# Three row normalisations from VectorE to ScalarE, with the shift made on GpSimd and a bias folded into a product

## The chip, the cores and the metric

The kernel runs on one core of a Trainium2 chip. Five engines work side by side, each with its own queue of instructions in a fixed order: TensorE (PE, with its weight loads as PEld), VectorE (DVE), ScalarE (ACT), GpSimd (POOL) and SyncE (SP), which issues most DMAs. They meet through semaphores: an instruction waits until a counter has reached a value. The metric is device time in microseconds (us) for one execution, as the median of the runs shown.

## The reference

Two blocks in a row, on 16 sequences of 256 tokens with 128 features, all fp32. The first is a state-space ("mamba") block with a residual and a row normalisation; the second is two transformer layers with attention in windows of 64 and a gated feed-forward; a residual and a last row normalisation follow. Cut to what matters here:

```python
# block 1
u = silu(conv(x @ in_w + in_b)); delta = softplus((u @ dt1_w + dt1_b) @ dt2_w + dt2_b)
h = A_bar * h + Bu            # scan over 256 tokens, 16 states, 256 channels
y = (einsum(hs, C_mat) + D_vec * u) * silu(x @ gate_w + gate_b)
x = _layernorm(x + y @ out_w + out_b)                 # normalisation 1
# block 2, for each of two layers
q, k, v = split(shift_token(x) @ wqkv)                # then l2norm, rotary, windows, softmax
x = x + o @ wo
h = shift_token(x)
h = (h - mu) / sqrt(var + 1e-05) * lg + lb            # normalisation 2
a, g = split(h @ w1 + b1)
x = x + (a * gelu(g)) @ w2 + b2
# end: residual with the input of block 2, then
out = _layernorm(x + ...)                             # normalisation 3
```

## The kernel before

The 32 row tiles of 128 tokens are worked in 10 groups (`SIZES`), four groups of two tiles and six of four tiles. A group passes through block 1 (index `g`) and then twice through block 2 (index `f` counts the 20 pairs of layer and group in the order `QUAD`, index `q` the 64 single tiles in it). Work on several groups is interleaved: while the scans of group g run, tiles of earlier groups go through attention and feed-forward.

Nothing is scheduled at run time. Each engine has a table of steps (`PE_ORDER`, `ACT_ORDER`, `DVE_ORDER`, `POOL_ORDER`, `SP_ORDER`), and runs them in that order. A step such as `ffn_norm 13` is a small function that waits on semaphores and issues a few instructions. Two further tables (`PAIR_TABLES`, `BANK_TABLES`) give the PSUM banks (AA, BB, YY in pairs, C and M single) that each step uses.

The three normalisations have the same shape, here for a group of two or four tiles:

- the statistics are made on DVE (`bn_stats`, `bn_aggr`, one pair for each tile), which give mean and variance of each row: steps `mamba_sum` (lines 1115 and 1120), `ffn_stats` (1205, 1210) and `final_stats` (1115, 1120);
- `mamba_rstd`, `ffn_rstd` and `final_rstd` on POOL add epsilon (line 774) and raise to the power -0.5 (line 776);
- `mamba_norm` and `final_out` (line 1125) and `ffn_norm` (line 1220) on DVE subtract the mean and multiply by the result, one `tensor_scalar` of 128x128 for each tile. Over the whole kernel these are 32 + 64 + 32 = 128 instructions in 40 steps.

Who waits for them: after `mamba_norm` PE transposes the rows (`layer_T`), after `ffn_norm` PE transposes (`norm_T`), ACT applies gain and offset of the layer (`norm_T` on ACT, line 957), and the up products follow; after `final_out` SP stores the group. `outb`, the tile in which a group's output is summed and normalised, exists once, so that `ffn_sum` of the second layer waits until the store of the group before has landed.

The bias of the down product is not in the product. The step `residual` on POOL adds it to the rows `x2` (line 812), and in the second layer adds the rows `x1` as well (line 815); `ffn_sum` on DVE then adds the product and waits for both.

`mamba_norm`'s DVE instruction, and the two POOL lines of the residual:

```python
ins = dve.tensor_scalar(dst[:, i, :], src[:, i, :], mv[:, i, 0:1], rs[:, i:i + 1],
                        ALU.subtract, ALU.mult)
pool.tensor_tensor(rows, rows, row("b2", g, l), ALU.add).then_inc(xb2_sb, 1)
pool.tensor_tensor(rows, rows, x1[:, g % X_RING, 0:tiles_of(g)], ALU.add).then_inc(xb1_sb, 1)
```

## Time and profile before

| what | value |
|---|---|
| median of three runs | 1025.17 us (1023.71 to 1028.51) |
| the profiled execution, device time | 1025.69 us |
| its span, first to last instruction | 1023.9 us |
| mean granted TensorE clock | 0.979 |
| busy PE / DVE / ACT / POOL | 906.2 / 890.3 / 788.3 / 701.1 us |

The profile gives for each engine the time in which at least one of its instructions ran. Matmuls overlap each other, and so do short ACT and DVE instructions that follow each other, so a sum of single durations can exceed the busy time. An engine's idle time is split by what ended it: the last semaphore that it waited for, or "issue" where the trace shows no such wait. The span is shorter than the device time of the same execution by 1.8 us.

### The profile page before, as it was taken

Reading aid. Unit: us, or ns where it says so; the run is one execution under the profiler, and the core shown is the slowest. Engines: PE = TensorE matmul, PEld = TensorE weight load, DVE = VectorE, ACT = ScalarE, POOL = GpSimd, SP = SyncE. Lnnn points to the kernel's source line nnn. Section 1 sums busy time; section 2 is a strip of 40 time slices with the busy share of each in tenths; the row PEclk is TensorE's granted clock in tenths of the full one; section 3 lists DMA queues with packets and bytes.
Section 4 is the critical chain, followed back from the end, with each engine's and each line's share of the span. In section 5 each row is a group of like instructions: output and inputs, shape, how many; then the busy total and the mean of one; then the engine's idle time right before and its main releaser. Section 6 shows DMA issues by size and latency. Waiting matters only on the chain. (4 is left out here: it accounts for less than half of the span.)

```text
span 1023.9 us, 26019 instructions
## 1 busy us (share of the span) xinstructions
PE 906.2 (89%) x10152; PEld 550.7 (54%) x10152; DVE 890.3 (87%) x1244; ACT 788.3 (77%) x1901; POOL 701.1 (68%) x386
## 2 busy tenths in 40 slices
PE   3767678999988898999899989999899999999985
PEld 1333335456455465646564555546565566676664
DVE  7798997999879997999899998999899997774643
ACT  4467766996888859977898759995987987778771
POOL 4062424998579984799588892999478497886651
PEclk9979889999999999999999999999999999999998
DMA  7000000000001100000101100100110000010000
GB/s 239 11 17 16 12 1 21 23 19 15 17 17 27 27 23 16 18 22 22 32 18 27 22 12 22 28 23 6 28 32 23 2 23 22 17 33 18 17 22 11
DMA packets 22618, 25.63 MB, mean 25 GB/s; under 512 B 2869, under 2 KB 14815, under 8 KB 22495
## 3 DMA queue, kind: packets, MB, share of 16 engines
q1 hardware_dynamic: 22207, 23.81, 9.0%
q8 instruction: 81, 1.33, 0.6%
q14 instruction: 42, 0.34, 0.1%
q10 hardware_dynamic: 288, 0.14, 0.0%
HBM read 9.26 MB, written 2.10 MB: 11 GB/s over the span
## 5 line engine op out<-in xcount | busy, mean ns | idle before, releaser
L1088 DVE TENSOR_TENSOR_SCAN scan<-du,decay 128x1028 f32<-128x1028 f32 (+1 forms) x160 | 315.0, 2004 | 2.8 <-issue 1.3
L793 POOL TENSOR_TENSOR rn<-ssc,expo 128x16 f32<-128x16 f32 x64 | 214.6, 3354 | 5.3
L884 ACT ACTIVATE decay<-delta,negA 128x1024 f32<-128x1024 f32 (+1 forms) x160 | 154.9, 997 | 43.3 <-DVE scan L1088 37.7
L1278 PE MATMUL YY<-scan,diag 64*64 64x512 f32 (+1 forms) x1280 | 148.1, 552 | 32.1 <-DVE scan L1088 31.7
L789 POOL TENSOR_SCALAR ssc<-ss 128x16 f32<-128x16 f32 x64 | 61.9, 967 | 152.7 <-DVE ss L1145 152.0
L798 POOL TENSOR_TENSOR qkc<-qkc,qks 128x1024 f32<-128x1024 f32 x64 | 163.0, 2547 | 0.5 <-DVE qks L1163 0.3
L802 POOL TENSOR_TENSOR qkc<-qkc,rn 128x1024 f32<-128x1024 f32 x64 | 143.5, 2242 | 5.0
L940 ACT ACTIVATE prob<-AA,nmax 128x128 f32<-128x128 f32 x240 | 84.5, 384 | 15.1 <-DVE nmax L1183 15.0
L940 ACT ACTIVATE prob<-BB,nmax 128x128 f32<-128x128 f32 x232 | 81.7, 381 | 17.3 <-DVE nmax L1183 14.9
L1145 DVE TENSOR_REDUCE ss<-sq 128x16 f32<-128x1024 f32 x64 | 77.2, 1206 | 15.1 <-ACT sq L903 15.1
L1278 PEld LDWEIGHTS YY<-scan,diag 64*64 64x64 f32 x1280 | 38.3, 139 | 94.5 <-DVE scan L1088 68.9
L1278 PE MATMUL BB<-wqkv,hT 128*128 128x512 f32 x124 | 60.5, 610 | 3.7 <-ACT hT L895 1.8
L1278 PE MATMUL AA<-wqkv,hT 128*128 128x512 f32 x112 | 54.9, 613 | 6.4 <-ACT hT L895 2.0
L940 ACT ACTIVATION_READ_ACCUMULATOR prob<-AA,nmax 128x1 f32 x240 | 53.7, 224 | 0.0
L1278 PEld LDWEIGHTS M<-v_even,probT 128*64 128x64 f32 x640 | 41.2, 140 | 20.8 <-issue 16.8
L940 ACT ACTIVATION_READ_ACCUMULATOR prob<-BB,nmax 128x1 f32 x232 | 51.2, 221 | 0.0
L1278 PE MATMUL M<-v_even,probT 128*64 128x64 f32 x640 | 46.6, 227 | 1.6 <-ACT v_odd L919 1.4
L1278 PE MATMUL M<-v_odd,probT 128*64 128x64 f32 x640 | 46.7, 228 | 0.0
L903 ACT ACTIVATE sq<-BB 128x512 f32<-128x512 f32 x62 | 35.8, 616 | 11.3 <-PE BB L1278 10.9
L1052 DVE SCALAR_TENSOR_TENSOR hu<-upre,pv,hu 128x512 f32<-128x512 f32 (+1 forms) x60 | 42.2, 704 | 2.1
L1278 PEld LDWEIGHTS C<-wo,oT 128*128 128x128 f32 x352 | 40.4, 192 | 6.5 <-issue 4.2
L1278 PE MATMUL C<-wo,oT 128*128 128x128 f32 x352 | 42.3, 277 | 1.8 <-DVE x L1245 1.5
(210 smaller groups left out, 2279.2 us busy)
## 6 DMA issues: line engine op xcount, KB each, us to landing
v_even<-v_odd SPq DMA_DIRECT2D x96, 128.0 KB, 2.3
x<-in_x SPq DMA_DIRECT2D x6, 256.0 KB, 3.3
wqkv<-in_wqkv SPq DMA_DIRECT2D x1, 1536.0 KB
xT<-in_xT SPq DMA_DIRECT2D x6, 256.0 KB, 2.7
out<-outb SPq DMA_DIRECT2D x6, 256.0 KB, 2.3
w<-in_w SPq DMA_DIRECT2D x1, 682.0 KB
xT<-in_xT SPq DMA_DIRECT2D x4, 128.0 KB, 2.5
x<-in_x SPq DMA_DIRECT2D x4, 128.0 KB, 2.9
```

The lines of the kernel that those rows point to most:

```text
L789: pool.tensor_scalar(ssc[:, :], ss[:, :], 1e-24, None, ALU.max).then_inc(ssc_sb, 1)
L793: pool.tensor_tensor(rn[:, q % 2, :], ssc[:, :], expo[:, 0:2 * HEADS], ALU.pow).then_inc(rn_sb, 1)
L798: pool.tensor_tensor(both_qk, both_qk, qks[:, q % 2].rearrange("p a x -> p (a x)"), ALU.add).then_inc(rope_add, 1)
L802: pool.tensor_tensor(all_heads, all_heads, rn[:, q % 2, :].unsqueeze(2).to_broadcast((P, 2 * HEADS, DH)), ALU.mult).then_inc(qk_sb, 1)
L884: act.activation(decay[:, at % A_RING, both(g), 1:], delta[:, both(g), :], ACT.Exp, scale=negA[:, n:n + 1]).then_inc(decay_sb, 1)
L903: act.activation(sq[:, a, :], bank_of("qk_in", q, a), ACT.Square).then_inc(sq_sb, 1)
L940: ins = act.activation(prob[:, h, :], bank_of("scores", q, a)[:, c * P:(c + 1) * P], ACT.Exp, bias=nmax[:, q % 2, h:h + 1], accum_out=den[ ...
L1052: dve.scalar_tensor_tensor(out=hu[:, ab(g, h), :], in0=upre[:, ab(g, h), c:c + SEQ], scalar=col("conv_w", k + c), in1=hu[:, ab(g, h), :], ...
L1088: dve.tensor_tensor_scan(state, step, a, 0.0, ALU.add, ALU.mult).then_inc(scan_sb, 1)
L1145: dve.tensor_reduce(ss[:, :], sq[:, :, :].rearrange("p a (h x) -> p (a h) x", x=DH), AX.X, ALU.add).then_inc(ss_sb, 1)
L1278: return pe.matmul(dst, lhsT, rhs, start=start, stop=stop, skip_group_check=True)
```

## The change

The three normalisations leave DVE and become ScalarE activations of the kind `Identity`, `scale * x + bias`, with scale and bias read from a column for each row. The scale is the power from POOL as before. The bias is -mean * scale, for which POOL makes two more small instructions in every `rstd` step (lines 782 and 786 of the changed kernel). `mamba_norm`, `ffn_norm` and `final_out` so stand in ACT's order and no longer in DVE's. The bias of the down product becomes row 86 of the third chunk of `w2`, against a row of ones in `hid`, and the third matmul of each tile contracts over 86 rows and no longer 85; `residual` keeps only the addition of `x1` in the second layer. All five order tables and both bank tables are written anew. The diff, cut to its core:

```diff
-for _name, _n in (("A_log", NST), ("out_b", D), ("qk_scale", LAYERS * 2 * DH), ("b2", LAYERS * D)):
+for _name, _n in (("A_log", NST), ("out_b", D), ("qk_scale", LAYERS * 2 * DH)):
...
-                             (w2[0:CH[2][1], :, 2, :], t["w2"][:, 2 * P:HID, :].rearrange("l p n -> p l n"))]:
+                             (w2[0:CH[2][1] + 1, :, 2, :], t["w2"][:, 2 * P:HID + 1, :].rearrange("l p n -> p l n"))]:
...
+            pool.memset(hid[:, NCH - 1, :], 1.0)
...
-            def rstd(dst, mv, ve, g, nth, aggr, var, done):
+            def rstd(dst, off, mv, ve, g, nth, aggr, var, done, used, left):
                 n = tiles_of(g)
                 pool.wait_ge(aggr, nth)
                 pool.tensor_scalar(ve[:, 0:n], mv[:, 0:n, 1], EPS, None, ALU.add).then_inc(var, 1)
+                if nth > 1:
+                    pool.wait_ge(used, nth - 1)
+                pool.tensor_scalar(off[:, 0:n], mv[:, 0:n, 0], -1.0, None, ALU.mult).then_inc(left, 1)
                 pool.wait_ge(var, nth)
-                pool.tensor_tensor(dst[:, 0:n], ve[:, 0:n], expo[:, 0:n], ALU.pow).then_inc(done, 1)
+                pool.tensor_tensor(dst[:, 0:n], ve[:, 0:n], expo[:, 0:n], ALU.pow).then_inc(left, 1)
+                pool.wait_ge(left, 2 * nth)
+                pool.tensor_tensor(off[:, 0:n], off[:, 0:n], dst[:, 0:n], ALU.mult).then_inc(done, 1)
...
-                pool.tensor_tensor(rows, rows, row("b2", g, l), ALU.add).then_inc(xb2_sb, 1)
-                if l == 1:
-                    pool.wait_ge(xb2_sb, f + 1)
-                    pool.tensor_tensor(rows, rows, x1[:, g % X_RING, 0:tiles_of(g)], ALU.add).then_inc(xb1_sb, 1)
+                pool.tensor_tensor(rows, rows, x1[:, g % X_RING, 0:tiles_of(g)], ALU.add).then_inc(xb1_sb, 1)
...
+            def normalise(dst, src, of, rs, g, sig):
+                for i in range(tiles_of(g)):
+                    ins = act.activation(dst[:, i, :], src[:, i, :], ACT.Identity, bias=of[:, i:i + 1], scale=rs[:, i:i + 1])
+                ins.then_inc(sig, 1)
+            def ffn_norm(f):
+                l, g = QUAD[f]
+                act.wait_ge(f_rstd, f + 1)
+                if f:
+                    act.wait_ge(hnT_ps, f)
+                normalise(hn, tiles(one("shift", f)[:, :]), f_of, f_rs, g, hn_sb)
...
-            def normalise(dst, src, mv, rs, g, sig):
-                for i in range(tiles_of(g)):
-                    ins = dve.tensor_scalar(dst[:, i, :], src[:, i, :], mv[:, i, 0:1], rs[:, i:i + 1],
-                                            ALU.subtract, ALU.mult)
-                ins.then_inc(sig, 1)
...
                 dve.wait_ge(f_stat, f + 1)
+                if f:
+                    dve.wait_ge(f_rstd, f)
...
                 dve.wait_ge(w2_ps, f + 1)
-                dve.wait_ge(xb2_sb, f + 1)
...
+                        n += c == NCH - 1
...
 DVE_ORDER = """
-differences 0, masks 0, step_size 0, tables 0, scan 0 0, scan 0 1, scan 0 2, scan 0 3, scan 0 4, scan 0 5, scan 0 6,
+differences 0, step_size 0, scan 0 0, scan 0 1, scan 0 2, scan 0 3, scan 0 4, scan 0 5, scan 0 6, masks 0, scan 0 7,
```

Three places show what the new tables do. The first is ACT at the end of group 0's scans: `decay` is a scan's input, `upre` the first product of group 1 (for the convolution on DVE), `hT` the transposed rows of group 0. Before:

```order
L884 ACTIVATE decay<-delta,negA 128x2x256 x16
L844 ACTIVATE upre<-YY,pv 128x256 x2
L894 ACTIVATE hT<-C 64x256
L895 ACTIVATE hT<-C 64x255
L859 ACT_TABLE_LOAD
```

and now:

```order
L891 ACTIVATE decay<-delta,negA 128x2x256 x16
L961 ACTIVATE x<-x,m_of,m_rs 128x128 x2
L851 ACTIVATE upre<-YY,pv 128x256 x2
L901 ACTIVATE hT<-M 64x256
L902 ACTIVATE hT<-M 64x255
L866 ACT_TABLE_LOAD
```

The two normalising instructions of group 0 stand ahead of `upre` of group 1 in ACT's queue.

The second is POOL at its end, from the next to last group's feed-forward: `f_` names belong to normalisation 2, `z_` names to normalisation 3. Before:

```order
L774 TENSOR_SCALAR z_ve<-z_mv 128x2
L776 TENSOR_TENSOR z_rs<-z_ve,expo 128x2
L774 TENSOR_SCALAR f_ve<-f_mv 128x2
L776 TENSOR_TENSOR f_rs<-f_ve,expo 128x2
L812 TENSOR_TENSOR x<-x,bv 128x256
L815 TENSOR_TENSOR x<-x 128x256
L774 TENSOR_SCALAR z_ve<-z_mv 128x2
L776 TENSOR_TENSOR z_rs<-z_ve,expo 128x2
```

and now:

```order
L779 TENSOR_SCALAR f_ve<-f_mv 128x2
L782 TENSOR_SCALAR f_of<-f_mv 128x2
L784 TENSOR_TENSOR f_rs<-f_ve,expo 128x2
L786 TENSOR_TENSOR f_of<-f_of,f_rs 128x2
L779 TENSOR_SCALAR z_ve<-z_mv 128x2
L782 TENSOR_SCALAR z_off<-z_mv 128x2
L784 TENSOR_TENSOR z_rs<-z_ve,expo 128x2
L786 TENSOR_TENSOR z_off<-z_off,z_rs 128x2
L822 TENSOR_TENSOR x<-x 128x256
```

Each power has got a negation ahead of it and a product behind it, the addition of the bias is gone, and the statistics of group 8's output are now worked behind those of group 9's last feed-forward.

The third is ACT at its end; `hnT` and `hid` belong to the feed-forward, `outb` to the output. Before:

```order
L957 ACTIVATE hnT<-C,pv 128x256
L966 ACTIVATE hid<-YY,pv 128x256 x2
L966 ACTIVATE hid<-M,pv 85x256
```

and now:

```order
L961 ACTIVATE hn<-M,f_of,f_rs 128x128 x2
L984 ACTIVATE hnT<-C,pv 128x256
L995 ACTIVATE hid<-AA,pv 128x256 x2
L995 ACTIVATE hid<-M,pv 85x256
L961 ACTIVATE outb<-outb,z_off,z_rs 128x128 x4
```

The four `outb` instructions are those of groups 8 and 9, two each; group 8's output is normalised behind the last gelu. On DVE before, group 8's output was normalised ahead of the last feed-forward's statistics. Over the whole program ACT has 58 table loads before and 55 now.

## Rows read from the trace of the kernel before

**Rows 1.** The page's part 1: busy time, share of span, instructions.
```profile
PE 906.2 (89%) x10152; PEld 550.7 (54%) x10152; DVE 890.3 (87%) x1244; ACT 788.3 (77%) x1901; POOL 701.1 (68%) x386
```
**Rows 2.** Stretches: start:end, length, busy of PE, PEld, DVE, ACT, POOL (instructions); clock, DMA.
```profile
0.00:200.00 200.00, 140.66 (x1295) 70.44 (x1296) 176.22 (x230) 133.21 (x258) 82.80 (x55) 0.92 0.15 44
200.00:850.00 650.00, 610.13 (x7012) 369.94 (x7011) 609.56 (x804) 538.70 (x1309) 508.36 (x252) 1.00 0.08 21
...
850.00:1000.00 150.00, 142.11 (x1781) 100.66 (x1779) 96.36 (x182) 113.82 (x332) 105.65 (x72) 0.99 0.09 22
...
400.00:500.00 100.00, 96.69 (x1091) 58.83 (x1091) 93.01 (x121) 81.23 (x199) 86.70 (x40) 1.00 0.09 21
```
**Rows 3.** PE's waits from 200 to 850 us: for whom, us, times, longest.
```profile
PE YY L1278 <- DVE scan L1088: 6.0, 6, 2.1
PE BB L1419 <- ACT prob L940: 3.3, 6, 1.2
```
**Rows 4.** ACT's longest wait in the same stretch.
```profile
ACT prob L940 <- DVE nmax L1183: 24.2, 13, 5.5
```
**Rows 5.** DVE's groups by line: busy us, mean ns, idle before and its releaser.
```profile
L1125 DVE TENSOR_SCALAR x<-x,m_mv,m_rs 128x128 f32<-128x128 f32 x32 | 14.2, 499 | 3.7 <-POOL m_rs L776 3.7
...
L1220 DVE TENSOR_SCALAR hn<-C,f_mv,f_rs 128x128 f32<-128x128 f32 x38 | 13.0, 399 | 0.4 <-POOL f_rs L776 0.4
...
L1125 DVE TENSOR_SCALAR outb<-outb,z_mv,z_rs 128x128 f32<-128x128 f32 x32 | 12.8, 457 | 1.3 <-POOL z_rs L776 1.3
...
L1220 DVE TENSOR_SCALAR hn<-M,f_mv,f_rs 128x128 f32<-128x128 f32 x26 | 8.9, 400 | 1.9 <-POOL f_rs L776 1.9
```
**Rows 6.** Line 1125 alone from 200 to 850 us: DVE busy (instructions).
```profile
200.00:850.00 650.00, 20.55 (x42) 1.00 0.08 21
```
**Rows 7.** Line 1220 alone in the same stretch.
```profile
200.00:850.00 650.00, 14.92 (x44) 1.00 0.08 21
```
**Rows 8.** Single durations on line 1125, ns: shortest/median/longest.
```profile
L1125 DVE TENSOR_SCALAR x<-x,m_mv,m_rs x32: 296/341/2248, 45.2 to 862.3; 128x128 f32<-128x128 f32 x32
```
**Rows 9.** ACT's groups by line and shape.
```profile
L966 ACT ACT_TABLE_LOAD x19 | 24.4, 1283 | 4.7 <-PE BB L1278 3.0 <-PE YY L1278 0.8 <-PE AA L1278 0.5
...
L966 ACT ACTIVATE hid<-BB,pv 128x256 f32<-128x256 f32 x10 | 4.2, 471 | 0.1
...
L957 ACT ACTIVATE hnT<-C,pv 128x256 f32<-128x256 f32 x6 | 3.6, 601 | 10.4 <-PE C L1504 10.4
...
L864 ACT ACTIVATE dt_s<-YY,pv 128x128 f32<-128x128 f32 x4 | 1.5, 382 | 0.9 <-PE YY L1278 0.9
```
**Rows 10.** POOL's groups by line.
```profile
L812 POOL TENSOR_TENSOR x<-x,bv 128x512 f32<-128x512 f32 (+1 forms) x20 | 26.9, 1347 | 24.5 <-DVE hn L1220 24.5
...
L774 POOL TENSOR_SCALAR f_ve<-f_mv 128x4 f32<-128x4 f32 (+1 forms) x20 | 9.3, 467 | 45.5 <-DVE f_mv L1210 44.8
```
**Rows 11.** Timeline after group 0's scans: start, duration, what [idle before].
```profile
44.12 0.84 ACT L844 ACTIVATE upre<-YY,pv 128x256 f32<-128x256 f32 x2 [6.81 <-PE YY L1278]
...
45.15 0.60 DVE L1125 TENSOR_SCALAR x<-x,m_mv,m_rs 128x128 f32<-128x128 f32 x2 [1.14 <-POOL m_rs L776]
...
45.67 0.41 DVE L1048 TENSOR_SCALAR hu<-upre,pv 128x256 f32<-128x256 f32 x1
```
**Rows 12.** Timeline of the last 17 us.
```profile
1007.67 0.22 POOL L774 TENSOR_SCALAR f_ve<-f_mv 128x2 f32<-128x2 f32 x1 [1.70 <-DVE f_mv L1210]
1007.98 0.72 POOL L776 TENSOR_TENSOR f_rs<-f_ve,expo 128x2 f32<-128x2 f32 x1
1008.73 0.73 DVE L1220 TENSOR_SCALAR hn<-M,f_mv,f_rs 128x128 f32<-128x128 f32 x2 [1.14 <-POOL f_rs L776]
...
1013.82 0.47 ACT L966 ACTIVATE hid<-M,pv 85x256 f32<-85x256 f32 x1 [0.38 <-PE M L1278]
...
1018.11 0.42 DVE L1245 TENSOR_TENSOR outb<-M,x 128x256 f32<-128x256 f32 x1 [1.70 <-PE M L1278]
...
1020.48 0.60 DVE L1125 TENSOR_SCALAR outb<-outb,z_mv,z_rs 128x128 f32<-128x128 f32 x2 [1.14 <-POOL z_rs L776]
```

More of the change, by code:

```diff
@@ L782, in mamba_rstd @@
             def mamba_rstd(g):
-                rstd(m_rs, m_mv, m_ve, g, g + 1, m_aggr, m_var, m_rstd)
+                rstd(m_rs, m_of, m_mv, m_ve, g, g + 1, m_aggr, m_var, m_rstd, x1_sb, m_left)
             def scale(q):
@@ L1117, in stats @@
                 dve.wait_ge(stat, n)
+                if g:
+                    dve.wait_ge(rstd, g)
                 dve.memset(tick[:, :], 0.0)
```

555 lines of the change are left out of this document (275 added, 280 removed).

## The prediction, made before the changed kernel had run

> **What bounds the kernel now.** I read the busy times first. Over the span PE is busy 906.2 us and DVE 890.3 us, ACT 788.3 us and POOL 701.1 us [rows 1], but an average over 1023.9 us hides that the limits change, so I cut the span into stretches [rows 2]. The reader is to compare, in each row, the length with the busiest engine. From 0 to 200 us DVE is busy 176 us and PE only 141: the first groups run through scans with little else to do, and DVE sets the pace. From 200 to 850 us PE (610.1) and DVE (609.6 of 650 us) are level at 94%, ACT is at 83% and POOL at 78%. From 850 to 1000 us the scans are over; PE is at 95% and DVE at 64%. The last 24 us are one chain from engine to engine. So a load taken off DVE pays fully in the first stretch, partly in the second, where PE has only 39.9 us of idle to give back, and not in the third.
>
> Then I asked whom PE waits for in the second stretch. The longest entry is the scan on DVE with 6.0 us, the next the softmax exponentials on ACT with 3.3 us [rows 3]; no single cause comes near the 39.9 us. It is idle in many small pieces, from both engines. ACT in turn waits there for DVE's row maxima, 24.2 us [rows 4], which DVE reaches late because its queue is full.
>
> **The change, part by part.**
>
> *DVE loses the 128 normalising instructions.* Their busy time is 14.2 + 13.0 + 12.8 + 8.9 = 48.9 us [rows 5], of which 20.55 + 14.92 = 35.5 us lie from 200 to 850 us, in 42 + 44 = 86 instructions [rows 6, 7]. In the first 200 us fall the eight tiles of groups 0 to 2 and the first four of the feed-forward; at 0.30 and 0.37 us a tile (0.60 us for two [rows 11], 0.73 us for two [rows 12]) that is 3.9 us. The remaining 9 us or so lie behind 850 us, beside a DVE with room.
>
> One part of the 35.5 us is less sure than it looks. The normalisations that read SBUF take 0.30 us at the shortest and 2.25 us at the longest [rows 8], while those that read PSUM have a mean of 0.40 us [rows 5]; something holds the first kind up at times. Undisturbed, the 64 of them would be 64 x 0.30 = 19 us and not 27.0 us. If the hold-up passes to the next DVE instruction, 8 us of the 48.9 us, and some 6 us of the 35.5 us, are not saved.
> The Trainium skill says why this could be so (page "SBUF — State Buffer", section "Who interferes with whom"): VectorE and GpSimd share one pair of ports, the one that issues second blocks for the whole instruction of the other, and that holds for a tensor_scalar in a two-port mode as for any VectorE instruction with two SBUF inputs, which the scan is. By this rule the lower saving is the right one, and by the row alone the full one. The trace agrees in that only the form that reads SBUF has the long cases [rows 5, 8].
>
> *ACT gains them.* No row shows an Identity of 128x128 with both a scale and a bias from a column. The nearest: one column operand at this size takes 382 ns, and a second column operand costs 601 - 471 = 130 ns at 128x256 [rows 9]. That gives 512 ns for one. Two that follow each other overlap: two upre of 0.47 us take 0.84 us [rows 11], so each further one in a step adds 0.10 us less, 412 ns. With 24 steps of four tiles at 1.75 us and 16 of two at 0.92 us the sum is 42.0 + 14.8 = 57 us. If the second operand costs nothing it is 24 x 1.23 + 16 x 0.66 = 40 us. I take 57, since the row with both operands is the nearest kind; 86/128 of it, 38 us, comes in the second stretch. The new table has three table loads less, 3 x 1.28 = 3.8 us [rows 9], some 2.6 us of it there. ACT in the second stretch then has 538.7 + 38 - 2.6 = 574 us of work. DVE has 609.6 - 35.5 = 574 us as well, and PE still 610 us. The change so levels ACT and DVE below PE.
>
> *POOL* loses the 20 bias additions, 26.9 us, and gains 80 small instructions, between 0.22 us [rows 12] and 0.467 us [rows 10] each, 18 to 37 us. With 508 of 650 us busy [rows 2] this changes nothing as load. It does as delay: the negation stands between epsilon and power, and the product behind the power waits for it. From the gap of 0.09 us between two POOL instructions that depend on each other [rows 12] I get 0.25 us for the first and 0.31 us for the second, 0.55 us on each normalisation's way. It can be twice that in the second stretch (0.467 us in place of 0.22 us), where PE has other work in its queue.
>
> *PE* contracts over 86 rows where it had 85, in the same number of matmuls with the same columns: zero. What ffn_sum no longer waits for is an addition that was ready long before: zero. The new waits of the statistics for the rstd step of the group before, and of POOL for ACT's last normalisation, concern steps a group old: zero. The row of ones is one memset at the start, beside PE's wait for its weights: zero. On DVE the masks and tables move from ahead of the first scan to between scans. It is the same work on the same engine before the same last scan, so I take zero, though it may close or open an idle time of a microsecond or two.
>
> *Start.* Now the order counts. ACT normalises group 0 ahead of upre of group 1. Before, upre came at 44.12 us, while the normalisation on DVE ran only at 45.15 us, when the power was there; the convolution followed at 45.67 us [rows 11]. Now upre stands behind a wait until 45.15 + 0.55 = 45.7 us and 0.92 us of normalising, and the convolution, which needs the first half of upre, starts near 47.1 us: 1.4 us later, on DVE's path. For groups 1 and 2 upre stands ahead. The start gains 3.9 - 1.4 = 2.5 us; I take 2.
>
> *End.* The chain of the last group passes two normalisations. Each is later by 0.55 us on POOL and by 0.92 us on ACT against 0.73 and 0.60 us on DVE [rows 12]: 0.74 + 0.87 = 1.6 us. Group 8's output now stands behind the last gelu, which ends at 1014.29 us; normalised at 1015.2 us and stored in the 2.8 us that the last store takes (from 1021.08 us, the end of the last row of [rows 12], to the span's end at 1023.9), it frees outb at 1018.0 us, just ahead of the sum that needs it at 1018.11 us. Zero, up to 0.5 us.
>
> *Middle.* Between nothing and all of the idle time. With the load as it is PE reaches 96.7% in its best 100 us [rows 2]; at that share 610.1 us of work take 631 us, a gain of 19 us. This is one bound, and zero is the other. I take about half, 10 us (PE at 95.3%), because DVE gives up 35.5 us but ACT, which PE waits for nearly as often as for DVE [rows 3], takes 38 us.
>
> **The sum.** -2 - 10 + 0 + 1.6 = -10.4 us against the profiled execution, 1025.69 us: 1015.3 us. Its time lies 0.5 us above the median of the runs shown, so 1015 us against 1025.2 us.
>
> **The rivals.**
> 1. *DVE was the true limit.* PE's gaps are the echo of a DVE that is never free: the 24.2 us that ACT waits for row maxima [rows 4] speak for it. Then PE fills to 96.7% and the middle gives 19 us: -2 - 19 + 1.6, 1006 us. Against it: PE's own waits for DVE are few [rows 3].
> 2. *PE is the limit and nothing is hidden behind DVE.* The middle stays at 650 us; -2 + 1.6 gives 1025 us. For it: level busy times at 94% [rows 2], idle in small pieces. The new bank tables may also shift the small pieces either way.
> 3. *ACT's queue becomes the limit, slower.* ACT has 111 us of idle in the second stretch, 24.2 us of it waits for one result of DVE [rows 2, 4]. If such waits are latencies that stay, and do not shrink as work is added, the 36 us of net work lengthen the stretch, in the worst case in full. It decides as soon as less than 36 us of the 111 can be filled; with a third of the added work uncovered the middle grows by 12 us, and the time is 1037 us. The place is ACT's order, in which a normalisation waits for POOL with exponentials and copies for PE queued behind it, as in the start above.
>
> **How the numbers follow.** The forecast, 1008 to 1020 us, gets 0.40. Rival 1 gets 0.20, rival 2 0.24, rival 3 0.16. A measurement of this kernel can tell about 0.5%, 5 us, from no change. Faster by more (below 1020 us) are the forecast and rival 1: 0.60. Within it (1020 to 1030 us) is rival 2: 0.24, and slower is rival 3: 0.16. For a range that holds 8 times in 10 I cut the outer part of rival 1 and the outer half of rival 3: 1001 to 1034 us.
>
> **What would show it.** In the profile of the changed kernel: DVE busy near 841 us if the hold-ups go, 849 us if they pass on; ACT near 841 us; the new activations near 0.41 to 0.51 us; PE near 906 us, with its share in the middle at 95%. The convolution of group 1 should start about 1.4 us later than before relative to the statistics of group 0, and the last normalisation about 1.6 us later relative to the last attention output. I am wrong if PE's share in the middle stays at 94% or if ACT's activations turn up at the top of PE's waits. A middle that shrinks by over 19 us would say that PE's best stretch was no bound.

## The result, and the profile of the changed kernel

The changed kernel takes 1055.12 us (median of four runs, 1054.6 to 1055.62) against 1026.84 us (1023.71 to 1029.07) for the kernel before: a ratio of 1.0278, 95% interval 1.0245 to 1.031. It is slower by 2.8%. I had forecast 1015 us, with 1034 us as the upper end.

The page's part 1 of the changed kernel, under [rows 1]:

```profile
PE 927.4 (88%) x10152; PEld 556.6 (53%) x10152; DVE 839.4 (80%) x1116; ACT 826.3 (78%) x2026; POOL 690.2 (65%) x447
```

Set against [rows 1], the work itself moved almost as forecast: DVE lost 50.9 us, ACT gained 38.0 us, POOL lost 10.9 us. The span is 1053.8 us, 29.9 us longer. Of these PE is busy for 21.2 us and idle for 8.7 us. Its instructions are the same 10152. In the kernel before 36.4 us of PE's busy time lie at the lower of TensorE's two clock levels (1.2 GHz, half of 2.4 GHz), in the changed one 72.8 us. At half speed half of the difference, 18 us, is lost, so 18 of the 21.2 us are slower matmuls. The stretches of the changed kernel, in the columns of [rows 2], show where:

```profile
0.00:200.00 200.00, 148.56 (x1266) 70.48 (x1266) 158.13 (x213) 132.36 (x255) 85.47 (x62) 0.85 0.15 43
200.00:850.00 650.00, 598.25 (x6722) 360.42 (x6722) 565.64 (x694) 545.12 (x1348) 477.69 (x280) 0.98 0.08 20
850.00:1000.00 150.00, 143.21 (x1775) 98.43 (x1775) 96.40 (x157) 120.49 (x349) 107.24 (x80) 1.00 0.09 21
400.00:500.00 100.00, 89.15 (x908) 52.51 (x907) 86.64 (x75) 75.65 (x179) 78.20 (x34) 0.96 0.09 21
```

The middle row is the one to read. In the same 650 us PE gets through 6722 instructions where it had got through 7012: 4% less of the kernel is done. Its share is 92%, not the 95% I wanted to see. DVE fell from 94% to 87%. ACT went from 538.7 to 545.1 us only, because less of the kernel fits in. Between them no engine is now busier than 92%. The granted clock is 0.98 there against 1.00, and 0.85 against 0.92 in the first 200 us. A mean of 0.85 means 30% of the stretch at the lower level.

Who waits for whom in the middle, ACT's longest entry (as [rows 4]) and PE's longest ones (as [rows 3]):

```profile
ACT prob L947 <- DVE nmax L1204: 23.5, 16, 5.0
```
```profile
PE AA L1425 <- ACT prob L947: 4.2, 5, 1.6
PE BB L1425 <- ACT prob L947: 3.6, 2, 2.8
PE C L1284 <- ACT oT L957: 2.9, 4, 0.9
PE AA L1284 <- ACT hnT L984: 2.7, 4, 1.1
```

ACT's wait for DVE's row maxima was 24.2 us and is 23.5 us, though DVE is busy 44 us less in the stretch (some 35 us of that are the normalisations, and less of the kernel fits in). And ACT now heads PE's list, where the scan on DVE had stood with 6.0 us. It does so with its exponentials, not with the new activations.

The new activations, ACT's groups by line (busy us, mean ns of one, idle before):

```profile
L961 ACT ACTIVATE hn<-M,f_of,f_rs 128x128 f32<-128x128 f32 x42 | 16.2, 488 | 9.6 <-POOL f_of L786 9.6
...
L961 ACT ACTIVATE x<-x,m_of,m_rs 128x128 f32<-128x128 f32 x32 | 13.5, 507 | 8.3 <-POOL m_of L786 8.3
L961 ACT ACTIVATE outb<-outb,z_off,z_rs 128x128 f32<-128x128 f32 x32 | 13.4, 499 | 6.9 <-POOL z_off L786 6.9
```

One takes 0.49 to 0.51 us. The idle time before them looks like the price of waiting for POOL, but most of it isn't: 8.29 us of it is one wait at the start, which puts the convolution back by about 1.2 us (below), and 8.84 and 6.42 us are two in the tail, where ACT has nothing else to do. From 200 to 850 us ACT waits for POOL once, for 0.3 us.

The attention falls behind at one place. POOL's timeline (start, duration, idle before) has its longest idle time of the middle at group 4's entry into layer 0:

```profile
408.63 0.25 POOL L799 TENSOR_SCALAR ssc<-ss 128x16 f32<-128x16 f32 x1 [19.69 <-DVE ss L1166]
```

By itself this says little, since POOL idles for 18.91 us at 537 us too, and the kernel before has an idle time of 17.77 us at 632 us. The softmaxes say more. Softmax 18 starts at 381.4 us, 0.4 us later than in the kernel before; softmax 20 starts at 433.05 us, 16.1 us later, and softmax 21 is 19.9 us late. From there on they stay 8 to 34 us behind.

### The profile page after: what moved, and what is told of

It reads as the page before. It is cut to its first block, busy times and chain, and to the rows that moved or that the text cites. A ratio compares the mean times of both kernels' runs of the same rounds, so it can differ in the third digit from the quotient of the medians.

```text
span 1053.8 us, 26096 instructions
## 1 busy us (share of the span) xinstructions
PE 927.4 (88%) x10152; PEld 556.6 (53%) x10152; DVE 839.4 (80%) x1116; ACT 826.3 (78%) x2026; POOL 690.2 (65%) x447
## 4 chain that ended last, share of the span: by engine, by line
PE 24%; ACT 14%; DVE 6%; issue 5%; POOL 4%; ACTq 0%; DVEq 0%; POOLq 0%
PE M L1284 6%; PE C L1284 5%; ACT prob L947 5%; PE YY L1284 4%; PE AA L1284 3%; PE BB L1284 2%; DVE scan L1117 2%; DVE nmax L1204 1%; POOL rn L803 1%; ACT decay L891 1%; ACT probT L916 1%; POOL qkc L808 1%; ACT qkT L935 1%; ACT hid L995 1%; PE AA L1425 1%
## 5 line engine op out<-in xcount | busy, mean ns | idle before, releaser
L1117 DVE TENSOR_TENSOR_SCAN scan<-du,decay 128x1028 f32<-128x1028 f32 (+1 forms) x160 | 317.8, 2021 | 5.3 <-ACT decay L891 4.6
L799 POOL TENSOR_SCALAR ssc<-ss 128x16 f32<-128x16 f32 x64 | 47.8, 747 | 198.3 <-DVE ss L1166 197.7
L1284 PE MATMUL YY<-scan,diag 64*64 64x512 f32 (+1 forms) x1280 | 151.8, 568 | 15.3 <-DVE scan L1117 15.2
L947 ACT ACTIVATE prob<-BB,nmax 128x128 f32<-128x128 f32 x248 | 87.2, 387 | 20.4 <-DVE nmax L1204 20.0
L1166 DVE TENSOR_REDUCE ss<-sq 128x16 f32<-128x1024 f32 x64 | 77.1, 1205 | 27.2 <-ACT sq L910 27.0
L947 ACT ACTIVATE prob<-AA,nmax 128x128 f32<-128x128 f32 x224 | 78.7, 381 | 19.4 <-DVE nmax L1204 19.0
L947 ACT ACTIVATION_READ_ACCUMULATOR prob<-BB,nmax 128x1 f32 x248 | 56.4, 227 | 0.0
L779 POOL TENSOR_SCALAR f_ve<-f_mv 128x4 f32<-128x4 f32 (+1 forms) x20 | 11.1, 553 | 62.8 <-DVE f_mv L1233 62.2
L1284 PEld LDWEIGHTS M<-v_even,probT 128*64 128x64 f32 x544 | 35.1, 141 | 20.2 <-issue 16.3
L916 ACT ACTIVATE probT<-AA 128x1024 f32<-128x1024 f32 x36 | 37.4, 1040 | 10.6 <-PE AA L1425 10.4
L1183 DVE TENSOR_TENSOR qkc<-BB,rope_c 128x1024 f32<-128x1024 f32 x31 | 37.6, 1213 | 9.5 <-ACT sq L910 7.4
L1284 PE MATMUL M<-hnT,w 128*128 128x256 f32 (+3 forms) x88 | 40.3, 541 | 5.4 <-DVE hid L1241 3.4
L1284 PE MATMUL M<-v_even,probT 128*64 128x64 f32 x544 | 39.7, 228 | 3.7 <-ACT probT L916 2.1
```

The lines of the kernel that those rows point to most:

```text
L799: pool.tensor_scalar(ssc[:, :], ss[:, :], 1e-24, None, ALU.max).then_inc(ssc_sb, 1)
L916: act.activation(probT[:, :, :, :].rearrange("p w h x -> p (w h x)"), pair("probs_T", q)[:, :], ACT.Copy).then_inc(pT_sb, 1)
L947: ins = act.activation(prob[:, h, :], bank_of("scores", q, a)[:, c * P:(c + 1) * P], ACT.Exp, bias=nmax[:, q % 2, h:h + 1], accum_out=den[ ...
L1117: dve.tensor_tensor_scan(state, step, a, 0.0, ALU.add, ALU.mult).then_inc(scan_sb, 1)
L1166: dve.tensor_reduce(ss[:, :], sq[:, :, :].rearrange("p a (h x) -> p (a h) x", x=DH), AX.X, ALU.add).then_inc(ss_sb, 1)
L1183: dve.tensor_tensor(dst_c, src, cos, ALU.mult)
```

## The experiments

All ratios are to the kernel before, measured beside it. "Old order" means the order and bank tables of the kernel before, "new order" those of the changed kernel. 1% is 10.3 us.

### The change taken apart by order: e1, e2, e3

e1 has the new instructions in the old order. Each normalisation stands in ACT's order where ACT was when DVE used to begin it. e2 is the reverse: the new order, with the normalisations on DVE and the short way on POOL. e3 is the kernel before with the bias row alone. Against the changed kernel e1 differs in the order and bank tables alone: they are those of the kernel before, with the normalisations moved from `DVE_ORDER` to `ACT_ORDER`. The diff of e3 against the kernel before, cut:

```
+            pool.memset(hid[:, NCH - 1, :], 1.0)
...
-                pool.tensor_tensor(rows, rows, row("b2", g, l), ALU.add).then_inc(xb2_sb, 1)
...
-                dve.wait_ge(xb2_sb, f + 1)
```

> The new instructions (normalisations on ACT, bias row, extra POOL instructions) with the order and bank tables of the kernel before; each normalisation stands in ACT's table where ACT was, in the trace of before, when DVE started it. Theory M, the move itself costs (ACT's queue and the longer way over POOL): at least 20 of the 28 us come back as a loss, 1045 us or more. Theory T, the rewritten tables cost and the move does not: 1015 to 1032 us.

> The new tables and banks and the bias row, but the normalisations back on DVE with the short way over POOL; each stands in DVE's table where DVE was, in the trace of after, when ACT started it. Theory M: the loss goes, 1020 to 1035 us. Theory T: it stays, 1048 us or more.

> The kernel before with only the bias of the down product as a row of it, so without 20 additions on POOL (26.9 us). Nothing waits for POOL there: within 0.3% of before, 1023 to 1030 us, by every theory. If the 86 rows or the missing port time mattered, it would show here as over 5 us.

e1: 1081.8 us, ratio 1.0518 (1.0476 to 1.0559). e2: 1082.25 us, 1.0531 (1.0502 to 1.0559). e3: 1027.15 us, 1.0007 (0.9988 to 1.0026).

The bias row is free, as forecast. Neither the new instructions nor the new order is harmless by itself: each alone costs about 5%. Theory M (the move costs) has e1 for it and e2 against it, theory T (the tables cost) the reverse, so these runs name neither as the culprit. With the new instructions the new order gives back 27 of the 55 us that they cost in the old one; with the normalisations on DVE it costs 56 us, though ACT and POOL then have no added work. The next runs ask why the move costs 55 us in the old order. What costs 56 us in e2 I didn't take apart.

### The clock: e4

e4 is the changed kernel with 20 further matmuls that are overwritten later, put ahead of four waits of 2 us and more (diff cut to two of the four):

```
+                if q == 5:
+                    warm(bank_of("probs_T", q, 0), 3)
...
+                if q == 21:
+                    warm(bank_of("qk_T", q, 0), 3)
```

> The changed kernel with extra matmuls whose result is overwritten, put into the four idle times of PE over 2 us in the stretch that PE bounds (before probs_T 5, up_gate 5, qk_T 21, shift 7), ahead of what PE waits for there. In the trace of after each of them is followed by 3.4 to 6.8 us at half clock. Theory C, the half clock costs the time: these windows go and the time falls by 8 us or more, to 1047 us or less. If the clock is only an echo of the waits: 1051 to 1058 us.

1053.93 us, ratio 1.0257 (1.0229 to 1.0284); the changed kernel has 1.0278. Three of the four drops in the granted clock behind the filled gaps went, one of them but for a short rest. The middle's clock rose from 0.98 to 0.99:

```profile
200.00:850.00 650.00, 602.29 (x6754) 359.00 (x6754) 564.62 (x694) 546.57 (x1353) 472.37 (x280) 0.99 0.08 20
```

In the same 650 us 32 more PE instructions fit in, but 20 of them are the fillers: 12 of the 290 that the changed kernel is short. In the middle the slower clock is mostly an echo of PE's waits. Between 394 and 440 us 4.5 us came back, but 3.8 us had been lost behind the first filler. What the lower clock of the first 200 us costs was not tried, and this stays open as a part of the loss. At 381 us the softmaxes are level with those of the kernel before, while the gating of group 4 on DVE comes 7.7 us late; how much of that is the clock stays open.

### Latency and load apart, in the old order: e5, e6

e5 keeps the normalisations on DVE and gives POOL the two further instructions. e6 keeps DVE's and POOL's instructions as they were and gives ACT 128 independent activations at e1's places. Both have the bias row and the changed kernel's wait of the statistics for the row scale of the group before. e6's added lines:

```
+                    act.activation(scratch[:, k % 4], ident[:, :], ACT.Identity, bias=col("gate_b", 0),
+                                   scale=col("gate_b", 1)).then_inc(loaded, 1)
```

> Order tables of the kernel before, normalisations on VectorE as before, bias row in the down product; only every row scale goes the changed kernel's longer way on GpSimd (two more small instructions, the shift -mean*rstd made though nothing reads it). 40 groups of normalisations each get their scale later by two GpSimd instructions. Theory A (the latency of the longer way is the cost): VectorE waits in its own order for the later scale, about 0.6 to 1.3 us each in 22 to 40 places, of which the old orders absorb little: 1042 to 1070. Theory B (the cost is ScalarE's order, where a normalisation that waits for GpSimd holds the exponentials and copies behind it): with ScalarE's order untouched nothing is lost: 1024 to 1032. Theory C (the old kernel has no slack for anything): between, about 1035.

> Order tables of the kernel before, normalisations on VectorE with the short GpSimd way, bias row; ScalarE gets 128 independent activations (128x128 from a constant tile to a scratch tile) at the places where the cross with the old tables had its normalisations. ScalarE's load without its waits; VectorE keeps all its work. Theory A (latency of the longer way) and theory B (in-order waits on ScalarE): most of the 55 us of the cross is missing: 1030 to 1045. Theory C (ScalarE's busy time as such, +60 us of it, is the cost since ScalarE has no slack around the exponentials): 1060 or more.

e5: 1034.83 us, ratio 1.0074 (1.0056 to 1.0092). e6: 1067.07 us, ratio 1.0406 (1.0378 to 1.0434).

Less the 0.7 us of e3, the latency costs about 7 us (3 us either way) and the load 41 us (4 us either way). e5 came to what theory C said, "about 1035", and e6 to its "1060 or more". Nobody waits for these 128 activations, and still they cost 84% of what they add to ACT's busy time (836.3 us against 787.7 us of e3). e6's page and the added group:

```profile
PE 919.6 (86%) x10152; PEld 556.8 (52%) x10152; DVE 893.5 (84%) x1244; ACT 836.3 (79%) x2029; POOL 671.1 (63%) x367
```
```profile
L1022 ACT ACTIVATE scratch<-ident,pv x128: 477/487/575, 44.9 to 1055.9; 128x128 f32<-128x128 f32 x128
```

ACT's idle time is 1023.9 - 788.3 = 235.6 us in the kernel before and 1065.0 - 836.3 = 228.7 us here. Of 48 us of added work ACT's idle time took in 7 us. The wait for the row maxima in the middle is hardly shorter either:

```profile
ACT prob L964 <- DVE nmax L1258: 22.1, 10, 4.6
```

### The three normalisations one by one: e7, e8, e9

Each has one normalisation on ACT with the long way on POOL, the others on DVE, in the old order. All three have the same kind of edit:

```
-            def final_out(g):
-                dve.wait_ge(z_rstd, g + 1)
-                normalise(outb, outb, z_mv, z_rs, g, out_sb)
...
+            def final_out(g):
+                act.wait_ge(z_rstd, g + 1)
+                normalise(outb, outb, z_off, z_rs, g, out_sb)
```

> Order tables of the kernel before; only the final normalisation (20 steps of the 40 groups' rows, 12.8 us of VectorE) as ScalarE activations with the longer GpSimd way, the two others on VectorE with the short way; bias row. Nothing waits for the final output but the store. Theory A and B both: ScalarE waits for the scale and delays the exponentials behind it: +5 to +20, 1032 to 1047, since each of the final steps is one place of the old order. Theory D (the cost is in the chains through the two inner normalisations, which feed TensorE): nothing lost, up to 8 us gained: 1018 to 1028.

> Order tables of the kernel before; only the feed-forward normalisation (20 steps, 64 tiles) as ScalarE activations with the longer GpSimd way. If the three normalisations add up (final 8 us, mamba 16 us, all three 55 us): 1050 to 1062. If the sum is more than its parts: 1035 to 1048.

> Order tables of the kernel before; only the mamba normalisation (10 steps, 42 tiles) as ScalarE activations with the longer GpSimd way; the two others on VectorE; bias row. Theory A and B: about a third to a half of the cross's 55 us, 1042 to 1055. Theory D (the chains through the inner normalisations): the same, since this one feeds layer 0's transposes and with them all of the attention. If it is under 1032, the cost must sit in the feed-forward normalisation or in the sum of the three.

Final (10 steps, 32 tiles): 1034.63 us, ratio 1.0074 (1.0047 to 1.0101). Mamba (10 steps, 32 tiles, where the expectation says 42): 1042.54 us, 1.0164 (1.0141 to 1.0187). Feed-forward (64 tiles): 1057.2 us, 1.0286 (1.0257 to 1.0315). e7 and e9 lie in the ranges of theories A and B, e8 in the one for costs that add up. The excesses sum to 5.24%; e1 has 5.18%. Even the final normalisation, for which nothing but a store waits, costs 8 us. That fits load on ACT again (13 us more busy time), though this run has the longer way on POOL too and doesn't separate the two.

My parts of e1 don't reach its 55 us, though: 41 for the load and 7 for the latency make 48, and DVE's relief should take some off. The traces show one more term. The scans on DVE, which no edit touched, take longer. In the kernel before, in e1 and in e8:

```profile
L1088 DVE TENSOR_TENSOR_SCAN scan<-du,decay 128x1028 f32<-128x1028 f32 (+1 forms) x160 | 315.0, 2004 | 2.8 <-issue 1.3 <-ACT decay L884 1.2
```
```profile
L1117 DVE TENSOR_TENSOR_SCAN scan<-du,decay 128x1028 f32<-128x1028 f32 (+1 forms) x160 | 333.6, 2121 | 3.3 <-ACT decay L891 1.6 <-issue 1.3
```
```profile
L1125 DVE TENSOR_TENSOR_SCAN scan<-du,decay 128x1028 f32<-128x1028 f32 (+1 forms) x160 | 332.8, 2116 | 3.5 <-issue 1.6 <-ACT decay L899 1.6
```

18.6 and 17.8 us more for the same 160 instructions. In e7 and e9 they take 314.8 and 314.7 us. So in the old order it is the feed-forward normalisation's move that shifts something against the scans. The changed kernel doesn't have the term (317.8 us), but e2, the new order with no normalisation moved, has 328.8 us. The move isn't needed for it, then, and the new order isn't free of it by itself. That GpSimd's instructions on SBUF hold the scans up is my reading, and no run isolates it.

### What DVE's time is worth: e10, e11

e10 cuts the normalisations on DVE to 2 of 128 columns, e11 adds 128 independent instructions to DVE:

```
-                    ins = dve.tensor_scalar(dst[:, i, :], src[:, i, :], mv[:, i, 0:1], rs[:, i:i + 1],
+                    n = 2 if dst is not outb else cut("outb", i)
+                    ins = dve.tensor_scalar(dst[:, i, 0:n], src[:, i, 0:n], mv[:, i, 0:1], rs[:, i:i + 1],
```
```
+                    dve.tensor_scalar(scratch[:, k % 4], ident[:, :], col("gate_b", 0), col("gate_b", 1),
+                                      ALU.subtract, ALU.mult).then_inc(loaded, 1)
```

> The kernel before with the bias row, its three normalisations on VectorE cut to 2 of the 128 columns of each tile (106 to 128 short instructions; the rest of a tile keeps what it had): what taking 36 to 38 us of work off VectorE is worth by itself, with nothing added on ScalarE. Theory A (the prediction's: VectorE's work is what the middle waits for, about a third of what it loses comes back): 1010 to 1018. Theory B (ScalarE is the engine whose time counts, VectorE's relief is worth nothing): 1024 to 1029. VectorE as the true limit would give 1000 or less.

> The kernel before with the bias row and 128 further independent instructions on VectorE (128x128 from a constant tile to a scratch tile), one ahead of each normalised tile: the counterpart of the 128 activations on ScalarE that cost 41 us, about 40 us of VectorE. Theory B (ScalarE alone is sensitive): under 15 us lost, 1028 to 1040. Theory C (every engine of this order is worked to its limit at the time each step comes, and added work costs nearly its full length anywhere): 30 us or more, 1055 and up. Theory A agrees with the latter.

e10: 1023.42 us, ratio 0.9967 (0.9947 to 0.9987). e11: 1072.59 us, ratio 1.0426 (1.0391 to 1.0461). DVE's busy time in the two:

```profile
PE 902.3 (88%) x10152; PEld 548.6 (54%) x10152; DVE 875.5 (86%) x1244; ACT 787.9 (77%) x1901; POOL 679.1 (67%) x367
```
```profile
PE 924.2 (86%) x10152; PEld 559.5 (52%) x10152; DVE 935.1 (87%) x1372; ACT 791.7 (74%) x1901; POOL 671.6 (63%) x367
```

e10 didn't do what I had written. DVE is relieved by 889.6 - 875.5 = 14.1 us and not by 36 to 38 us, since a cut instruction keeps most of its duration:

```profile
L1133 DVE TENSOR_SCALAR x<-x,m_mv,m_rs 128x2 f32<-128x2 f32 x32 | 8.0, 314 | 3.5 <-POOL m_rs L776 3.5
```

The time lies between the ranges of theory A (1010 to 1018 us) and theory B (1024 to 1029 us). Against e3 it gains 0.0040 of 1026 us, 4.1 us: some 0.3 us for each microsecond taken off, with an interval of about 0.1 to 0.5. In the other direction the price is another one: e11 adds 935.1 - 889.6 = 45.5 us and costs 43 us more than e3, 0.95 for each. DVE's idle time is 1070.1 - 935.1 = 135.0 us where it was 133.6 us. It took in nothing.

So theory C was right on added work in the old order: neither engine hides much, though DVE has 134 us of idle time and ACT 236 us. Theory B, that ScalarE alone is sensitive, falls. Removed work returns about a third while the order stays.

### Load and latency in the new order: e12, e13, e14

e12 is the changed kernel with activations cut to 2 columns, e13 the changed kernel with the short way (the activation's shift is the mean itself), e14 both:

```
-                    ins = act.activation(dst[:, i, :], src[:, i, :],
+                    n = cut(name, i)
+                    ins = act.activation(dst[:, i, 0:n], src[:, i, 0:n],
```
```
-                pool.tensor_scalar(off[:, 0:n], mv[:, 0:n, 0], -1.0, None, ALU.mult).then_inc(left, 1)
...
-                pool.tensor_tensor(off[:, 0:n], off[:, 0:n], dst[:, 0:n], ALU.mult).then_inc(done, 1)
```

> The changed kernel with its normalisations on ScalarE cut to 2 of the 128 columns of each tile, the waits, the order and the longer GpSimd way as they are: ScalarE's new load shrinks to its fixed part, some 20 to 25 us less. If ScalarE's busy time is what costs the changed kernel its 29 us: 1030 to 1038. If it is the waits and the latency of the longer way: 1048 or more.

> The changed kernel without the two further GpSimd instructions of a row scale: the activation's shift is the mean itself, not -mean*rstd, so that a scale is ready one instruction and its wait earlier (40 groups); order and ScalarE's full load as they are. If the latency of the longer way costs in the new order what it cost in the old one (8 us): 1045 to 1050. If the new order, made for it, hides it: 1052 to 1056. If latency and in-order waits for GpSimd are what remains of the loss: under 1040.

> The changed kernel with both taken away, the two further GpSimd instructions and 126 of the 128 columns of each normalised tile. If load (10 us) and latency add up: about 1037 to 1042. If this comes to the time of the kernel before, 1025 to 1030, load and latency together are the whole loss; what stays above it is the price of an order that was made around them, with VectorE's 51 us of relief still unused.

e12: 1045.66 us, ratio 1.0172 (1.0145 to 1.0199). e13: 1053.51 us, 1.0247 (1.0218 to 1.0276). e14: 1045.69 us, 1.0172 (1.0147 to 1.0197).

The latency is worth 3 us at most in the new order, inside the uncertainty. e13 says 3 us and e14 against e12 nothing. The load is worth 0.0106, 11 us, for 12.5 us less on ACT (826.3 to 813.8 us): 0.87 for each, with an interval of about 0.5 to 1.2. The second such pair, e13 against e14, gives 7.7 us for 11.0 us (825.5 to 814.5 us), 0.70. e13 came in the range for "the new order hides the latency". e12 missed both of its ranges (1030 to 1038, or 1048 and more) and e14 both of its own (1037 to 1042, or 1025 to 1030), since I had counted on some 20 us less on ACT.

e14 isn't a kernel without load, as I had meant it. A cut activation still takes 0.39 us (e12's rows), so ACT's busy time stays 814.5 - 787.7 = 27 us above that of e3:

```profile
L970 ACT ACTIVATE hn<-M,f_of,f_rs 128x2 f32<-128x2 f32 (+1 forms) x42 | 12.0, 388 | 9.0 <-POOL f_of L786 9.0
```

At 0.87 that is 23 us, more than the 17.7 us that e14 is above the kernel before. Its excess therefore proves no cost of the new order by itself.

### One place of the new order altered by hand: e15

The steps at this place, in the changed kernel (-) and in e15 (+):

```
-ACT:  ffn_norm 5, u_in 5, norm_T 5, probs_T 18, mamba_norm 4, silu_gate 5, out_T 17, silu_u 5, layer_T 0 4
+ACT:  ffn_norm 5, mamba_norm 4, u_in 5, norm_T 5, probs_T 18, out_T 17, layer_T 0 4, silu_gate 5, silu_u 5
-PE:   gate_in 5, layer_T 0 4, out_T 17, up_gate 5
+PE:   layer_T 0 4, out_T 17, gate_in 5, up_gate 5
```

> The changed kernel with one stretch of its order altered by hand, around group 4's entry into layer 0: on ScalarE mamba_norm 4 ahead of u_in 5, out_T 17 and layer_T 0 4 ahead of silu_gate 5; on TensorE layer_T 0 4 and out_T 17 ahead of gate_in 5. In the changed kernel this stretch (385 to 435 us) takes the attention from level with the kernel before to 20 us behind it. If a single late hand-over here is what the order costs: softmax 20 comes 4 us or more earlier and the end with it, 1046 to 1052. If the order makes the time up or loses it again elsewhere: softmax 20 earlier, the end within 2 us of the changed kernel's 1055.

1051.57 us (1051.1 to 1051.71), ratio 1.0235 (1.0218 to 1.0253); the changed kernel has 1.0278. ACT's timeline there, changed kernel first, then e15:

```profile
385.44 1.51 ACT L961 ACTIVATE hn<-M,f_of,f_rs 128x128 f32<-128x128 f32 x4
386.80 1.30 ACT L851 ACTIVATE upre<-YY,pv 128x512 f32<-128x512 f32 x2
...
388.61 1.08 ACT L916 ACTIVATE probT<-BB 128x1024 f32<-128x1024 f32 x1
389.51 1.69 ACT L961 ACTIVATE x<-x,m_of,m_rs 128x128 f32<-128x128 f32 x4
391.21 1.28 ACT L866 ACT_TABLE_LOAD   x1
392.51 1.26 ACT L866 ACTIVATE gate<-YY,pv 128x512 f32<-128x512 f32 x2
393.66 0.60 ACT L957 ACTIVATE oT<-C 128x512 f32<-128x512 f32 x1
...
395.09 0.58 ACT L901 ACTIVATE hT<-M 64x512 f32<-64x512 f32 x1
```
```profile
384.65 1.51 ACT L962 ACTIVATE hn<-M,f_of,f_rs 128x128 f32<-128x128 f32 x4
386.02 1.66 ACT L962 ACTIVATE x<-x,m_of,m_rs 128x128 f32<-128x128 f32 x4
...
390.69 0.60 ACT L958 ACTIVATE oT<-C 128x512 f32<-128x512 f32 x1 [0.27 <-PE C L1482]
391.19 0.58 ACT L902 ACTIVATE hT<-M 64x512 f32<-64x512 f32 x1
```

`oT` comes 3.0 us and `hT` 3.9 us earlier. PE, which had waited for that `oT`, no longer has its gap of 2 us there, and the four matmuls behind it take half the time. Changed kernel, then e15:

```profile
394.41 3.75 PE L1284 MATMUL BB<-hnT,w 128*128 128x512 f32 x4 [2.00 <-ACT oT L957]
```
```profile
392.21 1.88 PE L1285 MATMUL BB<-hnT,w 128*128 128x512 f32 x4
```

The gap didn't vanish, it moved: e15's PE waits 3.86 us for ACT's `v_odd` at 399.7 us, and the granted clock is at its lower level from 399.0 us on, for as long (6.8 us) as in the changed kernel from 393.7 us on. The drop that the changed kernel has at 431 us is gone. Softmax 20 comes only 2.1 us earlier, less than the 4 us I had asked for, but softmax 21 comes 4.5 us earlier, and this stays: 4.3 us at softmax 63, 4.0 us at gelu 19. So it neither went as the first case said in full nor was it lost again. Five steps stood in another order on two engines; that gives 4 us of 1055, and nothing later takes it back. No complete version that I ran beats the kernel before. e10, which leaves work out, is the only one below it, by 0.3%.

## Why the prediction was wrong

**What held.** ACT's busy time rose by 38.0 us, and I had 57 less 3.8, 53 us. The new activations are busy for 51.8 us (the three groups above and `hn` from C, 8.7 us), since four in a row take 1.51 to 1.69 us and not 1.75 us. Less the 3.8 us of table loads that makes 48 us, 10 us more than ACT's busy time shows. ACT's other groups keep their durations (1.3 us less in sum), so the rest is mostly overlap of a new activation with its neighbour: in the timeline above `upre` starts at 386.80 us, before `hn` ends at 386.95 us. One activation at 0.48 to 0.51 us lies in my range of 0.41 to 0.51. DVE's 839.4 us match the 841 us for "the hold-ups go". The Trainium skill (page "SBUF — State Buffer", section "Who interferes with whom") says which VectorE and GpSimd instructions lock each other out. It doesn't say where a hold-up goes when one of them is taken away; that they pass to the next VectorE instruction with two SBUF inputs, which would have given 849 us, was my use of it. The trace of the changed kernel goes against this use, with scans of 317.8 us against 315.0 us. e1 and e8, with scans up by 18 us, show that the scans can take longer in another order; whether by such hold-ups no run says. The bias row cost nothing (e3).

The start: the convolution of group 1 begins 45.86 - 42.84 = 3.02 us after the last aggregate of group 0, against 45.67 - 43.86 = 1.81 us. That is 1.2 us later, and I had said 1.4 us. The start as a whole didn't come out, though. It was to gain 2 us; the first scan of group 1 starts 0.3 us earlier than before, that of group 2 at 110.52 us, 3.5 us later, and softmaxes 3 to 5 are 1.1 to 3.1 us late. The runs don't say why; the granted clock is lower there, 0.85 against 0.92.

In the kernel before, and then in the changed one:

```profile
43.86 0.15 DVE L1120 BATCH_NORM_AGGREGATE m_mv<-m_st 128x2 f32<-128x6 f32 x1
```
```profile
42.84 0.15 DVE L1151 BATCH_NORM_AGGREGATE m_mv<-m_st 128x2 f32<-128x6 f32 x1
```
```profile
43.56 0.71 POOL L784 TENSOR_TENSOR m_rs<-m_ve,expo 128x2 f32<-128x2 f32 x1
44.36 0.20 POOL L786 TENSOR_TENSOR m_of<-m_of,m_rs 128x2 f32<-128x2 f32 x1
44.59 0.88 ACT L961 ACTIVATE x<-x,m_of,m_rs 128x128 f32<-128x128 f32 x2 [8.29 <-POOL m_of L786]
45.37 0.81 ACT L851 ACTIVATE upre<-YY,pv 128x256 f32<-128x256 f32 x2
45.86 0.41 DVE L1077 TENSOR_SCALAR hu<-upre,pv 128x256 f32<-128x256 f32 x1 [2.87 <-ACT upre L851]
```

The end: from the last `f_ve` to the end of the last normalisation it takes 1050.89 - 1035.93 = 14.96 us, and took 1021.08 - 1007.67 = 13.41 us [rows 12]: 1.55 us more, forecast 1.6 us.

```profile
1035.93 0.23 POOL L779 TENSOR_SCALAR f_ve<-f_mv 128x2 f32<-128x2 f32 x1 [11.00 <-DVE f_mv L1233]
...
1050.01 0.88 ACT L961 ACTIVATE outb<-outb,z_off,z_rs 128x128 f32<-128x128 f32 x2 [6.42 <-POOL z_off L786]
```

**The step that failed** is the middle: "Between nothing and all of the idle time ... I take about half, 10 us". I saw 111 us of idle time on ACT there, took it as room, and set zero as the worst case of the move. In its place the changed kernel loses time in the middle: 4% less of the kernel is done from 200 to 850 us. What was missing from the sum is a price for work added to ACT. e6 measures 0.84 us for each microsecond in the old order and e12 0.87 in the new one, and e11 shows that it isn't a property of ACT (0.95 on DVE). That my 10 us for 35.5 us taken off DVE, 0.28, agrees with e10's 0.3 is luck: the 10 us were half of PE's room, with ACT's load already weighed in. With these rates the forecast would have read: ACT's measured 38.0 us at 0.87, 33 us; the end's 1.6 us; DVE's 50.9 us at 0.3, -15 us; latency 0 to 3 us. That makes about 20 to 23 us of loss, where 28 us were measured.

The size is near, but the place is not, and so the rates don't prove the cause in the changed kernel. Every kernel here runs the 160 scans in the same order, 16 for each group, so their starts can be set side by side. The start of a group's first scan in the kernel before (us), and how much later it comes in the others:

| first scan of group | 4 | 5 | 6 | 7 | 8 | 9 | end of span |
|---|---|---|---|---|---|---|---|
| before, at | 294.4 | 415.7 | 530.6 | 640.2 | 744.1 | 808.2 | 1023.9 |
| changed kernel | -3.5 | 2.8 | 23.3 | 24.9 | 27.2 | 22.6 | 29.9 |
| e12, new order, short activations | -5.4 | -0.4 | 14.8 | 15.7 | 16.3 | 11.5 | 17.4 |
| e2, new order, normalisations on DVE | -0.1 | 10.6 | 29.1 | 36.9 | 48.2 | 44.5 | 58.8 |
| e6, old order, load on ACT | 3.7 | 5.1 | 12.9 | 23.2 | 28.8 | 32.8 | 41.1 |

The rows of groups 5 and 6, in the kernel before and then in the changed one:

```profile
415.66 2.29 DVE L1088 TENSOR_TENSOR_SCAN scan<-du,decay 128x1028 f32<-128x1028 f32 x1
530.60 2.29 DVE L1088 TENSOR_TENSOR_SCAN scan<-du,decay 128x1028 f32<-128x1028 f32 x1
```
```profile
418.50 2.29 DVE L1117 TENSOR_TENSOR_SCAN scan<-du,decay 128x1028 f32<-128x1028 f32 x1
553.85 2.29 DVE L1117 TENSOR_TENSOR_SCAN scan<-du,decay 128x1028 f32<-128x1028 f32 x1
```

In e6 the lag grows all along. In the changed kernel 20.5 of 29.9 us arise between two marks, in the place where the softmaxes fall behind, and only 6.6 us behind them. Yet 76 of the 128 new activations stand behind the second mark, as many as in e6. ACT's busy time of the new activations from there on, in the changed kernel (line 961) and in e6 (`scratch`):

```profile
554.00:1053.00 499.00, 30.56 (x76) 0.99 0.09 21
```
```profile
543.40:1065.00 521.60, 31.71 (x76) 0.97 0.08 19
```

About 31 us of activations go with 28.2 us of added lag in e6, and with 6.6 us in the changed kernel, where DVE is relieved too. So from 554 us on the new order takes most of the load in. Between the two marks e2, which has no added load at all, loses 18.5 us, and e12 still loses 15.2 us. Most of the loss at this one place so seems to go with the new order, and not with the length of the new activations. The marks are scans alone, and the two orders put other work between them; the softmaxes agree on the place. e15 shows that a late hand-over there is worth 4 us of it. What the rest of it is stays open.

Why the idle time takes so little in, in the old order, is argued, not shown by a run of its own. Each engine runs its list in order, and each step waits for another engine: PE for ACT's exponentials, ACT for DVE's maxima, DVE for PE's scores. ACT's idle time is made of such hand-overs. A delay on ACT delays PE, PE delays DVE, and the hand-over comes later by the same amount, so the wait stays as long as it was. The traces agree in the part that can be read: ACT waited 24.2 us for the maxima before, 22.1 us in e6 and 23.5 us in the changed kernel. Idle time on ACT was 235.6, 228.7 and 227.5 us. This is agreement, not proof: the table above shows that the same mechanism costs little in the last half of the changed kernel.

**The rivals.** Rival 3 named this mechanism and its worst case ("if such waits are latencies that stay ... in the worst case in full") and gave it 0.16 and a third of its price. The third was a number of convenience, and with it the range ended at 1034 us. At its full price, 36 us in place of the forecast's -10 us, the same sum would have given 1061 us. Its place was wrong too: ACT doesn't stand waiting for POOL in the middle. Taking the longer way away gains 7 us in the old order (e5, the reverse) and 0 to 3 us in the new one (e13, e14). Rival 1 needed DVE to be the limit, and e10 speaks against it. Nor was DVE's full queue the reason for ACT's wait for the maxima, as I had read it: with DVE down from 94% to 87% the wait is 23.5 us where it was 24.2 us. Rival 2's premise, that what DVE gives up is worth little, holds in part. Its side remark, that the new tables may shift things either way, was worth more than I made of it, as e2 shows. My signs of being wrong did their work: PE's share in the middle fell to 92%, though ACT's head entry in PE's waits is the exponentials and not the new activations.

**The clock** was not in my forecast at all. PE was busy 21.2 us longer for the same instructions, 18 us of it by the lower clock. From 200 to 850 us the granted clock fell behind each of four waits of 2.00 to 2.79 us. In the kernel before two gaps of 2.12 and 2.14 us, at 294 and 502 us, were followed by no drop, so a gap's length alone doesn't decide. e4 puts the price in the middle at 1 to 5 us. For the first 200 us there is no such run.

## What to carry to other kernels

In a kernel whose engines run fixed lists and wait for one another in a ring, an engine's idle time is not room by itself. In an order not made for the added work, price it at nearly its full length (0.84 to 0.95 here, with 13 to 23% idle), and what is taken off at a third, until a run says otherwise. By these rates a move to the less busy engine pays only if the instruction becomes a good deal shorter there; the ones that read PSUM went from 0.40 to 0.49 us, the others from 0.46 and 0.50 to 0.50 and 0.51 us. An order made for the work can take most of it in, as the second half of the changed kernel does, and can lose 20 us at a single place. So look where the lag arises before you put it down to a rate: compare the start of the same instruction in both traces at some ten marks. Such a rate costs one run to measure: put the same number of independent instructions at the places where the new ones would stand.

## What the runs showed that I had not expected

- Cutting an instruction from 128 columns to 2 saves little. On DVE `x` goes from 499 to 314 ns, and on ACT `hn` from 488 to 388 ns. Most of the 128 normalisations' busy time goes with their number.
- The scans' total moves between 314.3 and 333.6 us with the order of instructions elsewhere. The added group on DVE in e11, whose operands are constant and all in SBUF, takes 0.29 us at the shortest and 2.38 us at the longest:

```profile
L1132 DVE TENSOR_SCALAR scratch<-ident,pv x128: 291/341/2381, 45.1 to 1067.0; 128x128 f32<-128x128 f32 x128
```

- The costs of three moves added up to the cost of all three within 0.1% of the time, closer than the measurement can tell (each ratio has an interval of 0.2 to 0.4% either way). I had thought an order would break at some point, or take the first ones for free.
